# A language-model layer of eight sequences on one core: the front end moved ahead, weight chunks loaded in pieces, two norms moved between engines

## The reference

```python
emb = concat(fine_embed_w[ids], softmax(loc_to_cluster_w.T[ids] + b) @ coarse_embed_w)
x1  = layernorm(emb)                        # "first norm", with an RMS norm on it: xn
q, k, v = rms(x1) @ (basis @ coeffs.T)      # per sequence
x2  = x1 + mem_scale * (((q @ k.T) * decay_w) @ v) @ o_w.T * mem_out_scale
xn2 = rms(x2)                               # "second norm"
h   = emb + x2 + op_scale * gelu(xn2 @ read_w @ channel_mix + bias) @ write_w.T * op_out_scale
x3  = layernorm(h)                          # "third norm"
gates = top-6 of softmax(x3 @ router_w.T + bias), normalized, with a capacity of 768 tokens per expert
out = h + sum over 64 experts of gate * (silu(x3 @ w_gate.T) * (x3 @ w_up.T)) @ w_down.T
        + mean over 2 shared experts of the same, without gates
```

## Time and profile before

| | us |
|---|---|
| time, median of 3 runs (lowest to highest) | 724.21 (720.36 to 725.76) |
| the profiled execution: its own time | 723.17 |
| its span, first to last instruction | 721.4 |
| busy: TensorE / VectorE / ScalarE / GpSimd | 680.7 / 538.7 / 449.1 / 417.8 |
| mean granted clock of TensorE | 0.988 |

### The profile page before, as it was taken

One profiled execution on the slowest core, in us unless ns is written; L12 is line 12 of the kernel. 1 busy time (PEld: TensorE's weight loads), 2 busy tenths in 40 slices (PEclk: granted clock), 3 DMA queues, 4 the chain that ended last, 5 costly groups with the idle time before them and its releaser, 6 DMA issues.

```text
span 721.4 us, 10633 instructions
## 1 busy us (share of the span) xinstructions
PE 680.7 (94%) x3245; PEld 550.1 (76%) x3245; DVE 538.7 (75%) x1190; ACT 449.1 (62%) x789; POOL 417.8 (58%) x353
## 2 busy tenths in 40 slices
PE   7878798999999999999999999999999999999998
PEld 7766476778877887878778788778778788777885
DVE  4668687878778786877778787787778776786665
ACT  3335485676675676666765766766766747745554
POOL 5035677565655766555665756557565456656563
PEclk9999899999999999999999999999999999999999
DMA  5303634243333432333332433334333333344431
GB/s 201 128 1 96 197 105 126 89 128 105 113 101 96 136 112 96 110 113 114 103 117 81 141 108 103 99 114 122 113 100 105 110 106 117 100 109 140 139 124 51
DMA packets 49016, 80.59 MB, mean 112 GB/s; under 512 B 9536, under 2 KB 13760, under 8 KB 48960
## 3 DMA queue, kind: packets, MB, share of 16 engines
q1 hardware_dynamic: 47936, 77.83, 34.6%
q0 software_dynamic: 1024, 2.10, 1.5%
HBM read 76.75 MB, written 3.15 MB: 111 GB/s over the span
## 4 chain that ended last, share of the span: by engine, by line
PE 57%; DVE 13%; issue 11%; POOL 10%; ACT 4%; DMA 2%; SPq 0%; POOLq 0%; DVEq 0%; ACTq 0%
POOL hid L1153 8%; PE bank_u L506 5%; PE bank_u L508 5%; PE bank_u L507 5%; PE bank_y L499 5%; PE bank_y L497 5%; PE bank_y L496 5%; PE bank_g L507 5%; PE bank_g L506 5%; PE bank_g L508 5%; DVE bank_u L996 4%; DVE hid_lo L1002 2%; DMA gate_rows<-gates_dram 2%; ACT hid_hi L714 2%; DVE taken L936 1%
## 5 line engine op out<-in xcount | busy, mean ns | idle before, releaser
L1153 POOL TENSOR_TENSOR hid<-hid,gate_rows 128x512 f32<-128x512 f32 x256 | 337.8, 1322 | 251.9 <-ACT hid L706 236.0
L714 ACT ACTIVATE hid_hi<-bank_u 128x512 fp32r<-128x512 f32 x258 | 154.0, 597 | 214.4 <-DVE bank_u L996 205.1
L1002 DVE TENSOR_TENSOR hid_lo<-bank_u,hid_hi 128x512 fp32r<-128x512 f32 x258 | 177.5, 688 | 101.8 <-ACT hid_hi L714 98.7
L996 DVE TENSOR_TENSOR bank_u<-hid,bank_u 128x512 f32<-128x512 f32 x258 | 178.0, 690 | 47.5 <-PE bank_u L508 37.0
L706 ACT ACTIVATE hid<-bank_g 128x512 f32<-128x512 f32 x264 | 157.3, 596 | 6.8 <-PE bank_y L491 5.3
L506 PE MATMUL bank_u<-x_hi,up_hi 128*128 128x512 f32 x264 | 114.2, 433 | 0.0
L506 PE MATMUL bank_g<-x_hi,gate_hi 128*128 128x512 f32 x264 | 105.8, 401 | 2.9 <-ACT hid L706 2.8
L507 PE MATMUL bank_g<-x_hi,gate_lo 128*128 128x512 f32 x264 | 105.2, 399 | 0.0
L508 PE MATMUL bank_u<-x_lo,up_hi 128*128 128x512 f32 x264 | 105.1, 398 | 0.0
L508 PE MATMUL bank_g<-x_lo,gate_hi 128*128 128x512 f32 x264 | 104.6, 396 | 0.0
L507 PE MATMUL bank_u<-x_hi,up_lo 128*128 128x512 f32 x264 | 104.6, 396 | 0.0
(11 more groups left out here) (222 smaller groups left out, 816.6 us busy)
## 6 DMA issues: line engine op xcount, KB each, us to landing
gate_rows<-gates_dram SPq DMA_DIRECT2D x512, 128.0 KB, 2.9
out_dram<-later SPq DMA_DIRECT2D x7, 256.0 KB, 3.1
hid<-gate_t_dram SPq DMA_DIRECT2D x2, 704.0 KB, 5.8
raw<-down_t_dram SPq DMA_DIRECT2D x2, 704.0 KB, 8.4
gates_dram<-gates_t SPq DMA_DIRECT2D x8, 128.0 KB, 2.2
gate_rows<-up_t_dram SPq DMA_DIRECT2D x1, 704.0 KB, 5.7
later<-up_t_dram SPq DMA_DIRECT2D x1, 704.0 KB, 8.7
raw<-gate_t_dram SPq DMA_DIRECT2D x1, 704.0 KB, 10.9
```

Of the source, the lines that this page charges most:

```text
L714: act.activation(hid_hi[:, split_slot(b, p), :], bank_u[(PAIRS * b + p) % 3][:, :], ACT.Copy)\
L996: dve.tensor_tensor(u, h, u, ALU.mult).then_inc(sem("product"), 1)
L1002: dve.tensor_tensor(hid_lo[:, k, :], bank_u[(PAIRS * b + p) % 3][:, :], hid_hi[:, k, :].bitcast(F32), ALU.subtract).then_inc(sem("hid_lo"), 1)
L1153: pool.tensor_tensor(hid[:, s, :], hid[:, s, :], gate_rows[:, row, :], ALU.mult).then_inc(sem("gated"), 1)
```

## The change

*Places.* The late steps move ahead by one to three pairs: xn from p = 31 and 32 to 24 and 26 of the sequence ahead, xn_t from 32 to 29, y from 1 to 31, z_scores from 3 to 1, mem from 7 to 5, x2 from 8 to 6, x3 from 19 and 20 to 18, x3_t from 20 to 19, and everything behind it by one. Among the early steps logits goes from 7 to 3, mv1 from 16 to 14. The gathers on GpSimd go from p = 1 to 4 to 21, 23, 25 and 27, for a sequence later. *Buffers.* xn_hi and xn_lo get tiles of their own, one each; to make room, decay_full lies in vals and ones_row beside taken. *Norms.* xn2 and x3 of the sequences from 1 on go from ScalarE (activation with scale, and bias) to VectorE (tensor_scalar), four instructions each; xn and x1 stay on ScalarE. *Chunks.* The first two down chunks are loaded in the startup instead of the last gate and the first down chunk; the three that reuse a tile come in six pieces of up to two tiles, one per p, between the gate rows. *Shared experts.* The factor 1/2, which GpSimd multiplied into two weight tiles, goes into product of p = 0.

```diff
-DVE_AT = dict(xn=-2, xn_lo=0, xn_dec=1, x1=1, y_lo=2, scores=4, state=6, x2=8, mv2=9, result=9, xn2=11, h2=16, bn3=16,
...
+DVE_AT = dict(xn=-5, xn_lo=-3, xn_dec=-2, y_lo=-1, scores=2, state=4, x2=6, mv2=7, result=8, xn2=9, h2=15, bn3=15,
...
-DENSE = {0: (0, 1), 1: (2, 3), 2: (4, 5), 3: (6, 7), 4: (), 5: (), 6: (), 7: ()}
+DENSE = {0: (-3, -2, -1), 1: (0, 1, 2), 2: (3, 4), 3: (5, 6, 7), 4: (), 5: (), 6: (), 7: ()}
-RELOADS = {6: (5, 7), 7: (3, 6), 8: (4, 17)}
+RELOADS = {6: (3, 8), 7: (4, 14), 8: (5, 20)}
+PIECES = 6
...
-          ("down", 2 * CHUNK, "own0", PAIRS + 17, PAIRS + 20))
+          ("down", 2 * CHUNK, "own1", PAIRS + 22, PAIRS + 23))
...
-        xn_hi, xn_lo = x3_hi, x3_lo
+        xn_hi, xn_lo = (sb(n, [P, SEQ], F32R) for n in ("xn_hi", "xn_lo"))
...
-        def reload_chunk(sp, k):
-
-            sp.wait_ge(sem(f"split_lo{RELOADS[k][0]}"), 1)
-            load_chunk(sp, k)
+        def reload_piece(sp, k, i):
+
+            n, p0, buffer, _, _ = CHUNKS[k]
+            if i == 0:
+                sp.wait_ge(sem("split_lo"), RELOADS[k][0] + 1)
+            c = slice(2 * i, min(2 * i + 2, CHUNK))
+            sp.dma_start(raw[buffer][:, c, :], sources[n][:, p0 + c.start:p0 + c.stop, :]).then_inc(sem(f"raw{k}"), 16)
...
-                    if b == 0 and p == at:
-                        reload_chunk(sp, k)
+                    if b == 0 and at <= p < at + PIECES:
+                        reload_piece(sp, k, p - at)
...
-            if b and p in ACT_AT["xn2"]:
-                act.wait_ge(sem("inv2"), b + 1)
-                scaled(act, xn2, x2, inv2[:, :], None, ACT_AT["xn2"].index(p)).then_inc(sem("xn2"), 1)
-            if b and p in ACT_AT["x3"]:
-                act.wait_ge(sem("inv3"), b + 1)
-                scaled(act, x3, h2[par], inv3[:, :], off3[:, :], ACT_AT["x3"].index(p)).then_inc(sem("x3"), 1)
...
-            if b == 0 and p == DVE_AT["xn2"]:
-                dve.wait_ge(sem("inv2"), 1)
+            if p == DVE_AT["xn2"]:
+                dve.wait_ge(sem("inv2"), b + 1)
                 for t in range(TILES):
                     last = dve.tensor_scalar(xn2[:, t, :], x2[:, t, :], inv2[:, t:t + 1], None, ALU.mult)
                 last.then_inc(sem("xn2"), 2)
...
-            if b == 0 and p == DVE_AT["x3"]:
-
-                dve.wait_ge(sem("inv3"), 1)
+            if p == DVE_AT["x3"]:
+
+                dve.wait_ge(sem("inv3"), b + 1)
                 for t in range(TILES):
                     last = dve.tensor_scalar(x3[:, t, :], h2[par][:, t, :], mv3[:, t, 0:1], inv3[:, t:t + 1],
                                              ALU.subtract, ALU.mult)
...
+            if p:
+                dve.tensor_tensor(o, h, u, ALU.mult).then_inc(sem(done), 1)
             else:
-                dve.tensor_tensor(u, h, u, ALU.mult).then_inc(sem("product"), 1)
+                dve.scalar_tensor_tensor(o, h, 1.0 / SHARED, u, ALU.mult, ALU.mult).then_inc(sem(done), 1)
...
-                    if p in GATHER_AT and b:
-
-                        gather(pool, b + 2, par, GATHER_AT.index(p))
+                if b + 3 < BATCHES and p in GATHER_AT:
+                    gather(pool, b + 3, 1 - par, GATHER_AT.index(p))
```

More of the change, by code:

```diff
@@ L49 @@
 GATE_AHEAD, SILU_AHEAD, POOL_AHEAD = 2, 1, 1
-GATHER_AT = (1, 2, 3, 4)
-DVE_AT = dict(xn=-2, xn_lo=0, xn_dec=1, x1=1, y_lo=2, scores=4, state=6, x2=8, mv2=9, result=9, xn2=11, h2=16, bn3=16,
[L56 to L62, removed]
+GATHER_AT = (21, 23, 25, 27)
+DVE_AT = dict(xn=-5, xn_lo=-3, xn_dec=-2, y_lo=-1, scores=2, state=4, x2=6, mv2=7, result=8, xn2=9, h2=15, bn3=15,
+              mv3=16, x3=18, x3_lo=20, router=21, prob=23, top=24, chosen=25, gates=26, taken=28,
+              logits=3, exp_sum=8, h=10, bn1=12, mv1=14)
+PE_AT = dict(xn_t=-4, y=-2, z_scores=1, state=3, mem=5, out=6, xn2_t=11, vals=12, op=14, x3_t=19, router=20, gates_t=27,
+             exp_t=7, coarse=9)
+ACT_AT = dict(xn=(-9, -7), xn_hi=-3, x1=(-5, -4), y_hi=-1, z=2, ffn_t=3, xn2_t=12, vals=13,
+              x3_hi=20, router_exp=22, cluster_exp=6, exp_t=8)
+POOL_AT = dict(inv2=8, hx=(10, 11), inv3=16, inv1=15)
 STORE_AT = 14
-BEFORE = -2
+BEFORE = -5
 SQUARES = ("basis", "q", "k", "v", "o", "read", "write", "mix")
@@ L72 @@
 CHUNK = 11
[L75 to L82, removed]
-          ("down", 2 * CHUNK, "own0", PAIRS + 17, PAIRS + 20))
+FIRST = -3 * PAIRS
+CHUNKS = (("gate", 0, "hid0", FIRST + 13, 0),
+          ("up", 0, "rows", FIRST + 13, 4),
+          ("gate", CHUNK, "hid1", -2, 11),
+          ("up", CHUNK, "later", 0, PAIRS + 4),
+          ("down", 0, "own0", 3, PAIRS + 5),
+          ("down", CHUNK, "own1", 4, PAIRS + 9),
+          ("gate", 2 * CHUNK, "later", PAIRS + 11, PAIRS + 12),
+          ("up", 2 * CHUNK, "own0", PAIRS + 17, PAIRS + 18),
+          ("down", 2 * CHUNK, "own1", PAIRS + 22, PAIRS + 23))
 FIRST_LOADS = 6
-RELOADS = {6: (5, 7), 7: (3, 6), 8: (4, 17)}
+RELOADS = {6: (3, 8), 7: (4, 14), 8: (5, 20)}
+PIECES = 6
 CHUNK_OF = {(n, p0): k for k, (n, p0, *_) in enumerate(CHUNKS)}
@@ L384, in pe_late @@
                 pe.wait_ge(sem("xn_lo"), b + 1)
[L385 to L387 removed]
+                pe.matmul(f1[:, :], qk_hi[:, :], xn_hi[:, :], start=True, stop=False)
+                pe.matmul(f1[:, :], qk_lo[:, :], xn_hi[:, :], start=False, stop=False)
+                pe.matmul(f1[:, :], qk_hi[:, :], xn_lo[:, :], start=False, stop=True).then_inc(sem("pe_y"), 1)
             if p == PE_AT["z_scores"]:
@@ L735, in act_sequence @@
                         act_early(act, b + 2, q)
-                    if first and q in (0, 1, 3):
-                        act_silu(act, 0, {0: 4, 1: 5, 3: 6}[q])
+                    if first and q in (-3, -2, 0):
+                        act_silu(act, 0, {-3: 4, -2: 5, 0: 6}[q])
+                    if first and q == -1:
+                        for k in ACT_AT["x1"]:
+                            act_late(act, 1, 1, k)
                 if early:
```

67 lines of the change are left out of this document (26 added, 41 removed).

## The result

The changed kernel takes 712.32 us (median of 4 runs, 711.69 to 712.38), the kernel before 723.14 us in the same comparison (720.36 to 725.76): ratio 0.985, 95% interval [0.981, 0.989]. It is 1.5% faster; 705 us were forecast, in a range of 695 to 715. The profiled execution has a span of 710.5 us and lasted 712.3 us.

A forecast was written before the change was run, and what follows sets the result against it. TensorE's own work was taken as the bound, its waits and sequence 0's losses as winnable. From 723.2: -8.3 (xn), -10.8 (x3), -8.5 (sequence 0), +4.7 given back, +0.3 startup, +4.8 over six sequences: 705.4 us, range 695 to 715.

The forecast's parts named there:

- the rival of the moved wait: VectorE, late after `taken`, makes TensorE wait for y or hid_lo: 720.4 us, half of that 713; chance 0.22 for 710 to 720.
- signs named: Profile after: sequence about 81 us, xn wait gone, x3 under 0.5, clock 1.00, gate-row wait under 5, VectorE 67 us.
- Gathers: nothing: Gathers on GpSimd moved from p = 1 to 4 to every second p from 21: no cost, TensorE waiting for none.
- the gates, at 0.2 with an upper end of 1.5: Router-to-gates chain, p = 21 to 27, without room: 0.2 us lost per sequence, between 0 and 1.5.
- third rival: Slower: x3's four VectorE instructions each held by a GpSimd multiply: 743 us, 734 without the clock; chance 0.06.
- x3 on VectorE: -10.8: Before x3's transposes: scaling on VectorE removes TensorE's 10.8 us of waits, leaving 0.3 us per sequence.
- xn earlier: -8.3: Before xn's transposes: ScalarE makes xn at p = 24 and 26, three p ahead, removing 8.3 us of waits.
- the 0.3 per sequence: y earlier, on TensorE at p = 31 soon after `taken`: 0.3 us lost per sequence, between 0 and 1.5.
- xn2: nothing: Four xn2 instructions on VectorE at p = 9 cost it 0.9 to 1.1 us, hidden by p = 10 and 11.
- the 4.7 us given back: Sequence 0 losses: state 1.3, cluster-weight transposes 1.0, gate matmul of 10 0.4, last down chunk's clashes 2.0 us.
- The gain of 8.5: Sequence 0: 2.8 us before a gate matmul, 2.4 before the cluster weights' transposes and 3.3 of clock can come back.
- all of it is hidden: Rival: VectorE has spare time and no new wait arises: 700.6 us, or 695.9 without sequence 0's clashes; chance 0.15.

## Why the prediction was right, and where it was not

The sign, the size class and the range held, 712 against 705. By sequence the 6.9 us between the forecast's 705.4 and the profiled 712.3 split so: sequence 0 took about 5.5 us more than the sum had, four middle sequences 0.9 us each more (82.1 against 83.3 - 2.8 + 0.8 = 81.2), the last two 2.4 us less together, startup and end together 0.3 us more. That the time fell in the range is in part luck. Its upper half stood for the rival of the moved wait (713 at half size), and a wait did move, to the gates, but not for that rival's reason: in the loop TensorE never waited for y. Of the signs named, those for xn, x3 and the clock at 86 to 92 came; GpSimd's wait for gate rows in sequence 0 stayed at 6.6 us (under 5 was said), the clock fell at other places, and VectorE was busy for 68.8 us in a sequence (67).

**Gathers: nothing.** This is the step that failed in the middle sequences, where the prediction said: "TensorE waits for no gather either way". No one waits for a gather, but a gather occupies GpSimd for 0.99 us, the multiply behind it moves, and a VectorE instruction that meets that multiply is held. Priced at 0 (and the gates, at 0.2 with an upper end of 1.5, for another reason), it costs 2.07 us in each of four middle sequences (82.11 against 80.04), 8.3 us, shown by the two runs in which the gathers alone move (712.3 to 703.9, 709.1 to 700.5). In the fifth, sequence 0, 0.7 of the 1.0 us of the gates wait stays when the gathers move; moving the last weight chunk takes that to 0.5, and the cause of the rest is open. The expectations had counted five. The mechanism itself stood in the third rival and in its rule: the Trainium skill (SBUF — State Buffer, Who interferes with whom) says that VectorE and GpSimd can exclude each other for whole instructions, where VectorE runs a tensor_scalar in a mode that uses both port pairs, and also where it has two inputs in SBUF. The trace agrees on both kinds, L908 (0.17 to 2.24 us) and L918 of the run without L908 (0.49 to 1.00 us). L847 of the earlier trace rows, on which the prediction leaned for tensor_scalar, has two inputs in SBUF and is of the second kind. It was weighed at x3 only, and not at each small instruction that the moved gathers would push the multiplies against.

**x3 on VectorE: -10.8.** The size was right, the cause was not. The wait left because mv1, inv1 and inv3 come one p earlier ahead of x3, as the run with these put back shows (+9.3 us); the engine makes no difference in a middle sequence. The row that said so was at hand: the 0.69 us behind GpSimd's off3 in the earlier trace rows, which the prediction read as ScalarE standing behind hid_hi. It had counted mv1's move, but as room for x3 on VectorE. The third rival, each of the four held, did not come: in each of the seven sequences of the loop the first alone is held, to 0.70 us, and the four take about 1.46 us together in place of 1.1.

**xn earlier: -8.3.** The wait left. The three p of distance were not needed for it; that xn now stands ahead of the hid_hi that waits behind `taken` was nearly enough (0.4 us per sequence is what the distance adds). y was waited for once, 0.6 us in the startup, as before the change: the 0.3 per sequence was nothing.

**xn2: nothing, and sequence 0.** This is the other step that failed. On VectorE xn2 and x3 cost 3 to 4 us, all in sequence 0, where VectorE also has the remainders (712.3 against 709.1; 703.9 against 700.5, of which xn2 and x3 have about half each): the waits before vals (1.8 us) and before the router (1.6 us) were in no term. Of the 4.7 us given back, the 1.3 for state was right, since its wait grew from 1.24 to 2.38 us, first before, then after:

```profile
69.92 0.46 PE L414 MATMUL bank_f<-z,shared 128*128 128x128 f32 x2 [1.24 <-DVE turns L827]
69.11 0.72 PE L419 MATMUL bank_f<-z,shared 128*128 128x128 f32 x2 [2.38 <-DVE turns L824]
```

What was left out is the clock behind it: the same matmuls take 0.72 us in place of 0.46. The last chunk's clash took 1.4 (2.0 forecast), and the 0.4 before the gate matmul of p = 10 is not in the list. The gain of 8.5 came in part. The waits before the gate matmul (2.8 to 1.1 us in the whole run, of which 0.6 lay in the startup both times) and before the cluster weights (2.4 to 0.9) shrank, but with the new ones TensorE stands still for 10.7 us of sequence 0, where it stood for 9.8. And of the 3.3 us for the clock little came back: the low at 86 to 92 is gone, those at 70 to 72 and 116 to 120 came with the waits ahead of them, and by the prediction's own count (TensorE's busy time in each 2 us, times what the clock lacks of 1.00) sequence 0 lost some 4 us before and some 3 after. That pieces did this was argued and fell: whole chunks give the same time.

**What a wait is worth.** With every wait gone a middle sequence takes 80.04 us, 3.23 less than before, where its waits were 2.8 us. So the case "all of it is hidden" was the true limit of the middle sequences, and still 0.4 us too high.

What stays open: whether logits at p = 5 are worth anything in the total (698.8 against 700.5, with intervals that meet), which of mv1, inv1 and inv3 freed x3, and what shortened GpSimd's wait for gate rows apart from the pieces.

## What to carry to other kernels

When work is moved to or within GpSimd, look at what it pushes there: a VectorE instruction that takes 0.2 us by itself and stands in a chain with no room can cost a whole GpSimd instruction or two (here L908, 0.17 to 2.24 us). A wait that disappears together with two edits has two possible causes; the idle time in brackets of the first late instruction ([0.69 <-POOL off]) pointed here to the one that matters, before any experiment. And a sequence in which some side work is missing is a free experiment: it showed 80.04 us before anything was run.
